# Test-time-training attention with a quantized FFN on one core: query read behind the filler matmuls, rounding addend written in the weight's place, and re-ordered ScalarE, GpSimd and VectorE work

## The reference, cut to what matters

```python
# x: 2048 x 512; 16 heads of 32; chunks of 16 tokens
def step(S, inp):                      # one chunk; S is 32 x 32 per head
    qi, ki, vi, ei = inp
    kh = ki @ S
    mu, rstd = mean(kh), rsqrt(var(kh) + EPS)
    kh_hat = (kh - mu) * rstd
    g = w * kh_hat + b - (vi - ki)
    gw = g * w
    v_new = (gw - mean(gw) - kh_hat * mean(gw * kh_hat)) * rstd
    A = where(tri, qi @ ki.T, 0) * ei
    qh = qi @ S - A @ v_new
    o = qi + _ln(qh, w, b)
    S = S - (ki * ei).T @ v_new        # the next chunk needs this
    return S, o
# attention: q = silu(x@Wq), k normalized, v, beta, scan over chunks,
#            gate, rms norm, @Wo, then layer norm and residual
# ffn: w.astype(float8_e4m3fn).astype(float32) for gate, up and down;
#      down(silu(gate(x)*gs) * (up(x)*us)) * ds, then layer norm and residual
```

## Time and profile before

| | |
|---|---|
| median of 3 runs | 868.01 us (867.11 to 868.35) |
| the profiled execution | 868.21 us, span 866.4 us |
| busy | PE 781.9 us (90%), DVE 667.6 (77%), ACT 513.6 (59%), POOL 477.9 (55%) |
| chain that ended last | PE 59%, DVE 16%, ACT 9%, POOL 8%, issue 5% |

### The profile page before, as it was taken

The page is one execution under the profiler, slowest core; times in us unless marked ns, Lnnn a source line. Parts: engine busy times, 40 slices in busy tenths (PEclk is TensorE's granted clock), DMA queues, the critical chain, the costliest instruction groups (busy, mean ns, idle before and its releaser), DMA issues.

```text
span 866.4 us, 24472 instructions
## 1 busy us (share of the span) xinstructions
PE 781.9 (90%) x9068; PEld 590.4 (68%) x9068; DVE 667.6 (77%) x2690; ACT 513.6 (59%) x1355; POOL 477.9 (55%) x851
## 2 busy tenths in 40 slices
PE   8877677588898999999999999999999999978896
PEld 4645454376666777777777686777777777767695
DVE  2677887887877888878887888778887888878444
ACT  1787676777677665655656475656565565632331
POOL 5455746565565656556565647565655656536200
PEclk9889998989999999999999999999999999999999
DMA  8011120211211001000100010000100010000000
GB/s 279 27 50 59 35 69 25 68 44 29 71 38 39 2 2 51 3 26 3 50 2 26 2 39 14 26 2 2 51 2 26 2 50 2 2 2 25 25 25 25
DMA packets 16727, 28.58 MB, mean 33 GB/s; under 512 B 3520, under 2 KB 3520, under 8 KB 16608
## 3 DMA queue, kind: packets, MB, share of 16 engines
q1 hardware_dynamic: 16608, 27.02, 9.9%
HBM read 22.82 MB, written 4.19 MB: 31 GB/s over the span
## 4 chain that ended last, share of the span: by engine, by line
PE 59%; DVE 16%; ACT 9%; POOL 8%; issue 5%; SPq 1%; DMA 1%; POOLq 0%; ACTq 0%; DVEq 0%
PE bank L668 18%; PE bank L452 11%; PE bank L701 8%; PE bank L644 4%; PE bank L615 4%; POOL rho L1293 3%; PE bank L466 3%; PE bank L592 3%; PE bank L601 3%; ACT BDq L999 2%; PE bank L486 2%; ACT BDk L961 2%; DVE work L1620 2%; PE bank L623 2%; PE bank L502 1%
## 5 line engine op out<-in xcount | busy, mean ns | idle before, releaser
L1293 POOL TENSOR_TENSOR rho<-sy,cst 128x2 f32<-128x2 f32 x128 | 89.7, 701 | 207.0 <-DVE sy L1593 207.0
L615 PEld LDWEIGHTS bank<-VX,BDkR 128*64 128x64 f32 x1024 | 45.1, 140 | 74.9 <-DVE VX L1629 34.3
L1636 DVE TENSOR_TENSOR SQ<-SQ,bank 128x128 f32<-128x128 f32 x128 | 36.7, 287 | 69.2 <-PE bank L615 68.2
L1016 ACT ACTIVATE qhR<-bank 128x64 f32<-128x64 f32 x128 | 28.6, 223 | 93.8 <-PE bank L623 93.6
L615 PE MATMUL bank<-VX,BDkR 128*64 128x64 f32 x1024 | 56.9, 233 | 29.3 <-DVE VX L1629 28.6
L975 ACT ACTIVATE BDkR<-kR,cst 128x128 f32<-128x128 f32 x256 | 81.6, 401 | 0.0
L701 PE MATMUL bank<-DW,fh 128*128 128x512 f32 x188 | 78.9, 420 | 1.2 <-DVE fl L1704 0.6
L961 ACT ACTIVATE BDk<-bank 32x256 f32<-32x256 f32 x124 | 46.5, 375 | 53.2 <-DVE kR L1535 44.8
L701 PE MATMUL bank<-DW,fl 128*128 128x512 f32 x188 | 75.1, 400 | 0.0
L1615 DVE SCALAR_TENSOR_TENSOR work<-work,rho,rR 128x32 f32<-128x32 f32 x256 | 53.2, 249 | 26.5 <-POOL rho L1293 25.1
L592 PEld LDWEIGHTS bank<-SQ,BDk 128*64 128x64 f32 x1024 | 45.9, 139 | 38.0 <-issue 35.6
(11 more groups left out here) (184 smaller groups left out, 2183.3 us busy)
## 6 DMA issues: line engine op xcount, KB each, us to landing
xt<-in_x SPq DMA_DIRECT2D x16, 256.0 KB, 2.9
x<-in_x SPq DMA_DIRECT2D x16, 256.0 KB, 2.9
out<-x SPq DMA_DIRECT2D x16, 256.0 KB, 2.0
yb<-in_gate_w SPq DMA_DIRECT2D x12, 256.0 KB, 2.6
yb<-in_up_w SPq DMA_DIRECT2D x12, 256.0 KB, 2.6
yb<-in_down_w SPq DMA_DIRECT2D x12, 256.0 KB, 2.6
Wk<-in_wk SPq DMA_DIRECT2D x1, 1024.0 KB, 7.9
Wv<-in_wv SPq DMA_DIRECT2D x1, 1024.0 KB, 9.6
```

Source lines behind the costliest of these rows:

```text
L615: ins = mm(dS[p, e], bdkr[:, gh, j % 4, p], VX[:, e], start=True, stop=True, skip_group_check=True)
L1293: tt(dst, src, cst[:, C_NH:C_NH + n], ALU.pow).then_inc(*one)
L1636: tt(S, S, dS.rearrange("p (g e) -> p g e", e=DH), ALU.add).then_inc(*scan_v.one("S"))
```

## The change

On PE the four query-read matmuls (qs) move, in every chunk of tiles 0 to 4 (those in which a unit is rounded), from behind kh to the end of the filler, just ahead of write_state. The rounding's addend is written where the rounded weight will stand (`place(u)`), the shift and the quantize read it there, and the next unit's first step waits for the addend (`s_magic`) and no more for the quantize. On ACT `diag_q` half 1 moves from behind the unit of chunk 1 to chunk 3 (tiles 1 to 3) or ahead of chunk 1's tail and unit (tiles 0, and 4 on), and the second `prep_BDk` of tiles 1 to 3 moves from chunk 5 behind the unit of chunk 6. On POOL `prep_b1` of these tiles moves ahead of the shift of chunk 6. In the drain DVE's and ACT's orders change. No instruction is added or taken away.

```diff
@@ -320,6 +320,11 @@
+        def place(u):
+            w, e = unit(u)
+            return (GW, UW, DW)[w][:, e:e + D]
         def quantized(third, n):
@@ -336,6 +341,10 @@
             return unit_at(t, j - 1)
+        def rounding(t):
+            return any(unit_before(t, j) for j in range(NC))
@@ -414,7 +423,7 @@
                     elif n == 3:
-                        sp.wait_ge(s_quant, UNITS)
+                        sp.wait_ge(s_magic, UNITS)
                     sp.dma_start(x1[n % 4][:, :], x_t[n]).then_inc(s_xr[n % 4], 16)
@@ -592,6 +601,10 @@
                 ins.then_inc(*scan_t.one("kh"))
+            def read_queries(n, j, s):
+                c = NC * n + j
                 if j % 4 == 0:
@@ -743,6 +756,8 @@
                         read_state(t, j, s)
+                    if scan and not rounding(t):
+                        read_queries(t, j, s)
@@ -834,6 +849,9 @@
                         idle(2, cst)
+                    if scan and rounding(t):
+                        read_queries(t, j, s)
                     if scan:
@@ -1074,7 +1092,7 @@
                 act.wait_ge(s_over, u + 1)
-                fn(wmg[:, :], wmg[:, :], ACT.Identity, bias=epses[:, 6:7]).then_inc(s_magic, 1)
+                fn(place(u), wmg[:, :], ACT.Identity, bias=epses[:, 6:7]).then_inc(s_magic, 1)
@@ -1088,7 +1106,7 @@
                         if u:
-                            act.wait_ge(s_quant, u)
+                            act.wait_ge(s_magic, u)
                         else:
@@ -1126,8 +1144,8 @@
                     tail_xf(n - 1, 0, p)
+                    ffn_silu(p - 1, 4)
                     tail_xc(n)
-                    ffn_silu(p - 1, 4)
                     ffn_fh(p - 1, 4)
@@ -1181,11 +1199,11 @@
                     if j == 1:
+                        if scan and not early(t):
+                            diag_q(t, 1, s)
                         if tail and not s:
...
                         from_weight(t, 1)
-                        if scan:
-                            diag_q(t, 1, s)
                         if prep:
@@ -1198,6 +1216,8 @@
                         from_weight(t, 3)
+                        if early(t):
+                            diag_q(t, 1, s)
                         if prep:
@@ -1214,6 +1234,8 @@
                         from_weight(t, 6)
+                        if early(t + 1):
+                            prep_BDk(t + 1, o, 1)
                         if prep and not early(t + 1):
@@ -1252,6 +1274,7 @@
                             prep_g1(t + 1)
+                        if prep and not early(t + 1):
                             prep_BDk(t + 1, o, 1)
@@ -1390,7 +1413,7 @@
                 pool.wait_ge(s_magic, u + 1)
-                tt(wst[u % 2][:, :], wmg[:, :], wst[u % 2][:, :], ALU.subtract).then_inc(s_shift, 1)
+                tt(wst[u % 2][:, :], place(u).bitcast(F32), wst[u % 2][:, :], ALU.subtract).then_inc(s_shift, 1)
@@ -1427,6 +1450,8 @@
                         tail_ra(t - 2)
+                    if j == 6 and early(t + 1):
+                        prep_b1(t + 1)
                     if scan and pool_free(t, j):
@@ -1470,7 +1495,7 @@
                             ffn_fl(*ffn[1])
-                        if prep:
+                        if prep and not early(t + 1):
                             prep_b1(t + 1)
@@ -1730,18 +1755,17 @@
                 if u:
-                    dve.wait_ge(s_quant, u)
+                    dve.wait_ge(s_magic, u)
                 ts(wmg[:, :].bitcast(I32), wst[u % 2][:, :].bitcast(I32), 0x7F800000, 0x00400000,
...
                 dve.wait_ge(s_magic, u + 1)
-                tt(wst[u % 2][:, :], wmg[:, :], wst[u % 2][:, :], ALU.subtract).then_inc(s_shift, 1)
+                tt(wst[u % 2][:, :], place(u).bitcast(F32), wst[u % 2][:, :], ALU.subtract).then_inc(s_shift, 1)
             def quantize(u):
-                w, e = unit(u)
                 dve.wait_ge(s_shift, u + 1)
-                tt((GW, UW, DW)[w][:, e:e + D], wmg[:, :], wst[u % 2][:, :], ALU.subtract).then_inc(s_quant, 1)
+                tt(place(u), place(u).bitcast(F32), wst[u % 2][:, :], ALU.subtract).then_inc(s_quant, 1)
@@ -1795,23 +1819,24 @@
                     end_og(0)
+                    ffn_f(p - 1, 2)
                     end_oss(0)
                     end_og(1)
-                    ffn_f(p - 1, 2)
                     end_oss(1)
...
                     fin_out(p - 2, 1)
+                    tail_x1(n - 1)
                     ffn_f(p - 1, 3)
+                    tail_stats(n)
                     ffn_fl(p - 1, 3)
-                    tail_x1(n - 1)
-                    tail_stats(n)
+                    ffn_f(p - 1, 4)
                     tail_x1(n)
-                    for r in (4, 5):
-                        ffn_f(p - 1, r)
-                        ffn_fl(p - 1, r)
+                    ffn_fl(p - 1, 4)
+                    ffn_f(p - 1, 5)
+                    ffn_fl(p - 1, 5)
                     pair_xl(p)
```

## The result

The changed kernel takes 854.25 us (median of 4 runs, 853.06 to 855.89) against 868.18 for the kernel before beside it: ratio 0.984, 95% interval 0.982 to 0.986. The prediction was 856.0, range 851.0 to 862.5. The profiled execution took 855.89 us with a span of 854.1.

The account below looks back on a forecast made before the run. PE was taken to bound tiles 5 to 15, PE's and DVE's waits on each other and on ACT and POOL tiles 0 to 4; 9.0 there plus 3.3 in the drain, 12.3 us off, gave 856.0, range 851.0 to 862.5.

Parts of the forecast that it names:

- End of tile 0, 2.4: Chunks 0.5 to 0.7: addend's new place ends ACT's quantize wait, PE's filler runs at full clock; 2.4 us, ends 1.1 and 2.8.
- Ends of tiles 1 and 2, 3.6: Chunks 1.5 to 1.7 and 2.5 to 2.7: DVE's wait for prep_b1 falls away; 2.0 and 1.6, together 3.6 us.
- Rival 2: Low clock stays in 0.6, 4.2 and the drain, as waits for VX replace waits for ACT; 859.7 us, chance 0.18.
- Chunks 2.2 and 2.3, 0.65: Only the shift's lag behind VX is gained, the rest becomes PE's wait for VX; 0.65 us, ends 0.5 and 3.9.
- Rival 1: All PE's waits come back: 3.9 us in 2.2, not 0.65, and full clock through tiles 0 to 4; 851, chance 0.15.
- Chunks 4.1 and 4.2, 1.7: diag_q runs inside ACT's wait for POOL, so silu and all that follows come earlier; 1.7 us, ends 0.8 and 2.4.
- Other short waits, 0.6: Chunks 0.2, 3.1, 3.6 and 4.0: 0.6 us in all, ends -0.5 and 1.5.
- Tiles 5 to 15, nothing: PE busy 490 of 506 us at full clock there, so the change leaves that stretch alone.
- Drain, 3.3: Round 4's silu ready before PE, 1.75 us, and no low clock behind it, 1.5; sum 3.3, ends 0.5 and 3.5.
- What is hidden: diag_q in chunk 3 of tiles 1 to 3 costs ACT 1.67 us under cover; ACT's late copy could hold the write.
- Rivals 3 to 5: 3: first wait only moves, 863.7 us, 0.11; 4: filler loses its clock, 873, 0.03; 5: does nothing, 868, 0.03.
- rival 5: The chain through DVE bounds everywhere and the drain loses in ffn_fl what it gains; 868 us, chance 0.03.

Follow-up runs that it names:

- e9: The kernel before, unchanged, profiled a second time: 865.22 us.
- e2: The changed kernel with the addend written to the working buffer again and the next unit waiting for the quantize: ratio 0.986, 856.9 us.
- e5: The changed kernel with prep_b1 and the second prep_BDk of tiles 1 to 3 at their old places: ratio 0.989, 857.8 us.
- e6: The kernel before with only the query read moved behind the filler in tiles 0 to 4: ratio 1.000.
- e1: The changed kernel with the query read back in front of the filler in every chunk: ratio 0.989, 858.2 us.
- e7: The changed kernel with ACT's square of k ahead of tail_xf in chunk 2 of tiles 0 to 4: ratio 0.982, 851.6 us.
- e8: The changed kernel with unused matmuls filling PE's waits in chunks 0.2, 1.3, 1.6, 2.2, 2.3 and 2.6: ratio 0.982, 852.1 us.
- e11: The kernel of e7 with POOL's tail_rf of tiles 2 and 4 ahead of chunk 2's shift and diag_q of tile 0 behind the unit: 0.980, 850.5 us.
- e3: The changed kernel with diag_q of the second half behind tail_xc again from tile 5 on: ratio 0.987, 856.6 us.
- e12: The kernel of e11 with the unused matmuls of e8 in PE's waits: ratio 0.980, 849.65 us.

## Why the prediction was right, and where it was not

The time was right, 1.75 us off, with the gain spread otherwise. That it came so close is in part luck: 4.1 and 4.2 gave 1.35 less than forecast and the ends of tiles 1 and 2 0.6 less, and a stretch that I had put at nothing gave 1.6. The mean of the two profiles of before and the four of the changed order gives 246.8 to 239.0 for tiles 0 to 4: 7.8 us, where I had 9.0. Then 1.6 between tiles 5 and 15, where I had nothing, and 3.9 in the drain, where I had 3.3.

*End of tile 0, 2.4.* Measured 3.1, 0.3 above the term's upper end, in every execution of the changed order. The gain is there, the step that I gave for it is not. I read the low clock in 0.6 as the cost (write 2.8 us behind VX) and the quantize's wait ahead of `prep_rT` as what removes it. By e9 the kernel before takes the same 12.85 us with 0.6 at the full clock, and behind the same wait of 1.46 us; so the wait did not decide the clock either. Behind chunk 0.6 stood the row addend, shift, b1, bx, start of 0.7, which had slack in the first profile only because 0.6 was long. e2, e5 and e6 agree: without the addend's place 0.2 is lost, without the early b1 and BDk 1.7, and the read alone gives -0.4. The rest of the 3.1 no single edit owns by these runs (e1, with the read in front again, loses nothing here). I had said that alone the move gives nothing here, which was right, but for the wrong reason.

*Ends of tiles 1 and 2, 3.6.* Measured 2.1 and 0.95. DVE's wait for b1 is gone in both and 2.7's start comes 1.2 us behind the keys' read, where it came 3.1 behind. The term was too large at the end of tile 2 because `post_wo` took not 3.63 us but 5.34:

```profile
155.23 0.45 PE L628 MATMUL bank<-VX,BDkR 128*64 128x64 f32 x8 [1.92 <-DVE VX L1654]
...
156.75 0.44 PE L601 MATMUL bank<-SQ,BDk 128*64 128x48 f32 x8 [0.86 <-DVE SQ L1661]
156.99 5.34 PE L657 MATMUL bank<-Wo,o 128*64 128x512 f32 x16
```

The granted clock was half while it ran:

```profile
158.00:160.00 2.00, 2.00 (x6) 0.60 (x4) 1.57 (x12) 1.94 (x4) 1.25 (x5) 0.50 0.49 131
```

PE's filler in 2.6 is done earlier now, its wait for VX is 1.92 us long, and the low clock falls on the next chunk. Rival 2 described this, for other places; e7 and e8, both with 2.7 at 4.95, price it at 1.6. The clock falling in another chunk was one of the prediction's own signs of being wrong, and it showed: in 2.7, and in the first profile in 1.7, where `post_wo` kept its clock in the kernel before.

*Chunks 2.2 and 2.3, 0.65.* Measured 0.65 between the first two profiles and 0.5 in the mean, and e7 confirms the row that I had named. Rival 1 hung on this and is out.

*Chunks 4.1 and 4.2, 1.7.* Measured 0.35. The step "all that follows, the shift included, comes earlier by about as much" failed. The shift waits for VX of 4.2, which ended 4.25 us behind the keys' read before and after. 4.2 is 2.0 us shorter and 4.3 1.7 longer:

```profile
235.50 0.81 ACT L1067 ACTIVATE xn<-x,nb_f,rs_f 128x512 f32<-128x512 f32 x1 [4.17 <-POOL nb_f L1325]
...
236.82 0.69 DVE L1544 TENSOR_REDUCE kss<-xn_dv_rT 128x16 f32<-128x512 f32 x1 [2.26 <-ACT xn_dv_rT L957]
...
238.02 0.23 DVE L1618 BATCH_NORM_STATS2 sy<-bank 128x6 f32<-128x68 f32 x1
```

It is the row of 2.2 once more; I had found it there and not looked for it two tiles on.

*Other short waits, 0.6.* What remains of tiles 0 to 4 is 0.8: 0.9 in 4.0 and 0.9 in tile 3, less 0.6 in 0.1 and 0.2 and some tenths elsewhere. In 0.1 and 0.2 `diag_q` ahead of the unit costs more than the read gives, where I had it take most of that gain (e11, with it behind the unit again, takes 1.4 back).

*Tiles 5 to 15, nothing.* The missed term. `diag_q` moves in every tile that is not early, up to the last, and I had followed it only where units are rounded. PE was busy 97% there, and the 1.6 us lay in the other 3%, in five gaps of 0.3, as e3 shows.

*Drain, 3.3.* Measured 3.9. The wait for `ffn_fl` of round 2 was 0.94 and not 1.5, and PE kept its clock, as forecast. By the waits 2.1 us came from there and the rest, 1.7, from the clock (1.5 forecast).

*What is hidden.* No run tests `diag_q` in chunk 3 by itself; 1.3 and 3.3 take 6.7 to 6.8 and 6.5 us in the kernel before and in the changed one, so no cost shows. ACT's copy held the write nowhere.

Rivals 3 to 5 are out; e6 shows that rival 5's mechanism, the row through ACT, POOL and DVE as the bound everywhere, was true of the kernel before for the read's edit. It is the edits in the other engines' rows that made it worth something.

## What to carry to other kernels

Ask of a wait that an edit frees what the next chunk's start stands behind, on every engine, in this execution and in one where the chunk ahead is shorter: an order may look slack only because something else was late. An edit in a loop is priced in every iteration in which its condition holds, in the stretch that looks full too. Where engines share the bound, undoing edits one by one says what each is worth in company, and only trying one alone says what it is worth by itself: 4.4 and 0 here.

## What the runs showed of the hardware

The same program with the same waits ran chunk 1.7 at the full clock in one execution and, for much of it, at half of that in another. The changed kernel's second profile, behind the same waits of 1.39 and 0.86 as in the first:

```profile
108.26 0.45 PE L628 MATMUL bank<-VX,BDkR 128*64 128x64 f32 x8 [1.39 <-DVE VX L1654]
...
109.78 0.44 PE L601 MATMUL bank<-SQ,BDk 128*64 128x48 f32 x8 [0.86 <-DVE SQ L1661]
110.02 3.65 PE L657 MATMUL bank<-Wo,o 128*64 128x512 f32 x16
```

In the first profile that group took 5.34 us; its windows, the first profile's and then the second's, differ in the granted clock, 0.50 and 1.00:

```profile
110.00:112.00 2.00, 2.00 (x6) 0.61 (x4) 1.79 (x14) 1.92 (x4) 1.05 (x3) 0.50 0.44 131
```

```profile
111.00:113.00 2.00, 2.00 (x12) 0.76 (x10) 1.78 (x13) 1.92 (x4) 1.05 (x3) 1.00 0.45 131
```

The kernel before shows the same in 0.6: low behind a wait of 1.47 us in its first profile, full behind one of 1.46 in e9. So the idle time right ahead is not by itself what decides; what does stays open here.

The Trainium skill, "TensorE: Matmul & The Clock Gate", "A second HAM failure mode", says of another kernel that PE idled briefly between groups of matmuls often enough to make the clock oscillate. The traces agree as far as the low stretches of 1.7, 2.7 and the drain go: each lies behind waits of 0.9 to 2 us. They don't show that such waits suffice.

Tiles 0 to 4 took 237.5 to 240.1 us in four executions of one order; the largest single piece is chunk 1.7, 6.52 us in the first profile and 4.82 in the others. In e11 and e12 the runs of one kernel lie 11 and 5 us apart. The slowest of e11 has the lowest mean clock (0.972), but the fastest (0.983) not the highest, so that the clock does all of it is not shown. A single chunk's time at such a place is no measure of an edit; the sum over it and the next is.

VectorE's quantize, a subtract of 128x512, took 0.66 to 0.73 us in 32 of the 36 units of the changed kernel. Beside a two-input operation of GpSimd of the same size it took 1.75 in e11's chunk 2.3, and 1.75 in the changed kernel at 39.14 us, beside one that started at 39.06.
